# Order of exponentials, penalties and signed scores in the second half's turns of a fused decoder kernel

## What is computed

```python
# top-k self attention, 16 heads of width 8, the 64 best of 128 keys per query
scores = jnp.einsum('bhqd,bhkd->bhqk', q, k) / np.sqrt(D_HEAD)
_, idx = jax.lax.top_k(scores, 64)
logits = jnp.where(knn_mask, scores, -jnp.inf)          # knn_mask set at idx
x = x + out_proj(softmax(logits) @ v)
# channel attention, twice (global, local): q, k, v are scaled and shifted rows
scores = jnp.einsum('bhdn,bhen->bhde', qh, kh) * scale  # 4 heads, 32 x 32 channels
x = x + 2.0 * (att_global + att_local) * wp + bp
# eight experts, all of them on every token
h = jax.nn.silu(x @ wg) * (x @ wu);  acc = acc + h @ wd
```

## Time and profile before

| | us |
|---|---|
| median of three runs | 1395.84 (1394.71 to 1397.26) |
| the profiled execution, its own time | 1398.07 |
| its span in the profile | 1396.3 |
| PE busy | 1046.0 (75%) |
| DVE busy | 961.9 (69%) |
| ACT busy | 679.3 (49%) |
| POOL busy | 474.8 (34%) |

### The profile page before, as it was taken

The page is one execution under the profiler, slowest core; times in us unless marked ns, Lnnn a source line. Parts: engine busy times, 40 slices in busy tenths (PEclk is TensorE's granted clock), DMA queues, the critical chain, the costliest instruction groups (busy, mean ns, idle before and its releaser), DMA issues.

```text
span 1396.3 us, 17900 instructions
## 1 busy us (share of the span) xinstructions
PE 1046.0 (75%) x5079; PEld 690.8 (49%) x5082; DVE 961.9 (69%) x3098; ACT 679.3 (49%) x1774; POOL 474.8 (34%) x461
## 2 busy tenths in 40 slices
PE   5888846655767278877575689778998865888999
PEld 4766713334445145554443344433444444666887
DVE  7555587987577887778878868545668678665332
ACT  4444437433666245665237634265667634633321
POOL 4333347410654144445237500333334403311100
PEclk9999957766878678887577789999998986989999
DMA  4100110000000000000010001011110120222343
GB/s 138 29 23 30 29 32 1 1 0 1 10 22 10 5 18 14 18 9 1 1 54 1 1 22 61 23 46 50 54 46 23 50 76 23 70 90 77 122 147 116
DMA packets 41762, 53.88 MB, mean 39 GB/s; under 512 B 6448, under 2 KB 20672, under 8 KB 41664
## 3 DMA queue, kind: packets, MB, share of 16 engines
q1 hardware_dynamic: 41488, 52.24, 12.0%
q0 software_dynamic: 176, 0.53, 0.1%
HBM read 51.71 MB, written 1.05 MB: 38 GB/s over the span
## 4 chain that ended last, share of the span: by engine, by line
PE 48%; DVE 28%; ACT 9%; issue 7%; POOL 6%; DVEq 1%; DMA 0%; POOLq 0%; SPq 0%; ACTq 0%
PE psum L1739 7%; PE psum L1750 6%; PE psum L1725 6%; PE psum L1816 2%; PE psum L1508 2%; PE psum L1484 2%; PE psum L1603 2%; PE psum L1327 2%; PE psum L1823 2%; PE psum L1466 2%; ACT far L1034 2%; PE psum L1404 2%; PE psum L1557 2%; POOL Wk L711 2%; DVE nmax L2131 1%
## 5 line engine op out<-in xcount | busy, mean ns | idle before, releaser
L2259 DVE TENSOR_TENSOR big<-psum,qe 128x512 f32<-128x512 f32 x106 | 72.9, 688 | 159.8 <-PE psum L1750 76.9
L1187 ACT ACTIVATE qe<-psum 128x512 f32<-128x512 f32 x106 | 62.3, 595 | 127.3 <-PE psum L1739 127.1
L1725 PE MATMUL psum<-big,wexp 128*128 128x256 f32 (+1 forms) x340 | 117.4, 461 | 0.0
L1034 ACT ACTIVATE far<-far,half_far,fmul 128x128 bf16<-128x128 bf16 x256 | 103.0, 488 | 22.9 <-DVE hit L2034 22.9
L2047 DVE MAX8 near<-Wk 128x8 f32<-128x128 f32 x512 | 103.0, 276 | 0.0
L668 POOL TENSOR_SCALAR veps<-mv 128x4 f32<-128x4 f32 x35 | 8.8, 252 | 267.0 <-DVE mv L1953 267.0
L766 POOL TENSOR_TENSOR Wk<-Wk,far 128x1024 f32<-128x1024 f32 x32 | 68.2, 2135 | 70.3 <-ACT far L1034 70.3
L1725 PEld LDWEIGHTS psum<-big,wexp 128*128 128x128 f32 x340 | 70.5, 207 | 31.0 <-issue 22.3
L1750 PE MATMUL psum<-xin,wexp 128*128 128x512 f32 x128 | 70.0, 630 | 13.7 <-DVE far L2259 8.3
L1404 PE MATMUL psum<-ident,Wk 128*128 128x128 f32 x256 | 48.6, 360 | 42.1 <-POOL Wk L711 39.3
L1739 PE MATMUL psum<-xin,wexp 128*128 128x512 f32 x128 | 77.7, 693 | 2.4 <-DVE vaug L2699 1.5
(11 more groups left out here) (359 smaller groups left out, 2867.5 us busy)
## 6 DMA issues: line engine op xcount, KB each, us to landing
wexp<-in_mg SPq DMA_DIRECT2D x48, 256.0 KB, 2.6
wexp<-in_mu SPq DMA_DIRECT2D x48, 256.0 KB, 3.0
wexp<-in_md SPq DMA_DIRECT2D x48, 256.0 KB, 3.1
w<-in_aw SPq DMA_DIRECT2D x8, 256.0 KB, 2.8
w<-in_w2a SPq DMA_DIRECT2D x8, 256.0 KB, 2.6
wqkv<-in_aw SPq DMA_DIRECT2D x8, 192.0 KB, 2.2
ctxt<-in_ctx SPq DMA_DIRECT2D x5, 256.0 KB, 4.2
xin<-in_x SPq DMA_DIRECT2D x4, 256.0 KB, 2.9
```

What stands on the lines that cost most here:

```text
L1034: ins = act.activation(far[t][:, hd, :], far[t][:, hd, :], ACT.Identity, bias=half_far[:, 0:1], scale=fmul[t][:, hd:hd + 1])
L1187: act.activation(sg_of[k >= EARLY][k % 2], bank(5 + k % 2), ACT.Silu).then_inc(silu_done, 1)
L1725: mm = pe.matmul(bank(4)[:, 0:w], wd[l % 2][:, c + j, :], hid_of[k >= EARLY][k % CH][:, j * w:(j + 1) * w], start=first and j == 0, stop=l ...
L2259: dve.tensor_tensor(hid_of[k >= EARLY][k % CH], bank(U_BANK[k]), sg_of[k >= EARLY][k % 2], ALU.mult).then_inc(hu_done, 1)
```

## The change

Five edits, all in turns 7 to 17. (1) `hidden` of the chunk of point 0 moves from point 2 to point 3. (2) On ACT, penalties leave points 0, 1 and 2 (six, six and four heads) and go to points 3 to 6, four heads each, behind `scores_out` of point 5 and ahead of that point's SiLU; the exponentials at points 1 and 2 so come right behind the maxima. (3) On POOL, `less_penalties` moves from points 3 and 4 to points 6 and 8. (4) In the turns with a pair's channel attention and penalties (12 and 14), `signed_scores` moves from point 0 to point 2 and waits for the queries' last step, `c_q`. (5) In the channel attention of the pairs, keys are scaled and shifted at r = -5 and -4, the row of line 823 is added at r = 6 in place of 4; for pairs 2, 3 and 4 the product of queries and keys moves from r = 5 to 4, its maximum and difference from 6 to 5, its exponential from 6 to 4 (point 2, ahead of the SiLU of the chunk of point 0). No arithmetic is changed.

```diff
@@ -157,7 +157,7 @@
 def hidden_point(t):
     if t < START2:
         return t + 1
-    return t if t >= TURNS * PTS else t + 2 if t % PTS < 2 else t + 1
+    return t if t >= TURNS * PTS else t + 3 if t % PTS < 2 else t + 1
 
 
 CHUNK_AT = chunk_points()
@@ -767,14 +767,18 @@
 
             def topk(b, p, half):
                 lo, hi = RANGES[half]
-                if p == 0 and lo <= b < hi:
+
+                pair = next((g for g in range(2, NG) if CH_START[g] == (b - 1) * PTS + 10), None)
+                if p == (0 if pair is None else 2) and lo <= b < hi:
+                    if pair is not None:
+                        pool.wait_ge(c_q, 4 * pair + 4)
                     signed_scores(b)
                 if p == 2 and lo <= b + 2 < hi and b + 2 > lo:
                     spread_keys(b + 2)
                 if p == 3 and lo <= b - 1 < hi:
                     spread_queries(b - 1)
-                if p in (3, 4) and lo <= b < hi:
-                    less_penalties(b, p - 3)
+                if p in (6, 8) and lo <= b < hi:
+                    less_penalties(b, (p - 6) // 2)
                 if p == 10 and lo <= b < hi:
                     maxima_in_parts(b)
 
@@ -804,7 +808,9 @@
 
             def channel(g, r):
                 x, w = x_of[g], GROUPS[g][1]
-                if r == 0:
+
+                key_scaled, key_shifted, based = (0, 2, 4) if g <= 1 else (-5, -4, 6)
+                if r == key_scaled:
                     if g == 0:
                         pool.wait_ge(ew_in, 32)
                     pool.wait_ge(ctxp_in, 16 * (g + 1))
@@ -814,11 +820,11 @@
                         pool.tensor_tensor(chk[k][:, 0:w, :], ctxp_of[g], bc(rowe[:, 4 + 2 * k, :], w), ALU.mult).then_inc(c_k, 1)
                 if r == 1:
                     post_rsqrt(2 * g + 1, w)
-                if r == 2:
+                if r == key_shifted:
                     for k in range(2):
                         pool.wait_ge(c_k, 4 * g + k + 1)
                         pool.tensor_tensor(chk[k][:, 0:w, :], chk[k][:, 0:w, :], bc(rowe[:, 5 + 2 * k, :], w), ALU.add).then_inc(c_k, 1)
-                if r == 4:
+                if r == based:
                     pool.wait_ge(n_h, 2 * g + 1)
                     pool.tensor_tensor(x, x, bc(rowe[:, 9, :], w), ALU.add).then_inc(c_xb, 1)
                 if r == 7:
@@ -1057,10 +1063,10 @@
                     maxima(b - 1)
                 if p in (1, 2) and lo <= b - 2 < hi:
                     exponentials(b - 2, p - 1)
-                if p in (0, 1, 2) and lo <= b < hi:
-                    penalties(b, (range(0, 6), range(6, 12), range(12, H))[p])
                 if p in (5, 7) and lo <= b + 1 < hi:
                     scores_out(b + 1, (p - 5) // 2)
+                if p in (3, 4, 5, 6) and lo <= b < hi:
+                    penalties(b, range(4 * (p - 3), 4 * (p - 2)))
                 if p in (8, 9, 10, 11) and lo <= b + 1 < hi:
                     signs(b + 1, range(4 * (p - 8), 4 * (p - 7)))
 
@@ -1173,7 +1179,7 @@
                         act.wait_ge(base_done, 4 * HALVES)
                     for k in range(2):
                         act.activation(chv_of[g][k], ctxTp[:, 0:w, :], ACT.Identity, bias=cole[:, 2 * k + 1:2 * k + 2], scale=cole[:, 2 * k:2 * k + 1]).then_inc(c_v, 1)
-                if r == 6:
+                if r == (4 if 1 < g < NG - 1 else 6):
                     act.wait_ge(c_sub, g + 1)
                     act.activation(se[:, 0:2 * w, :], se[:, 0:2 * w, :], ACT.Exp, scale=float(P) ** -0.5).then_inc(c_exp, 1)
                 if r == 11:
@@ -1689,7 +1695,7 @@
                     pe.wait_ge(ctxp_in, 16 * (g + 1))
                     pe.wait_ge(n_x, NX_AT["project", g])
                     transposes(bank(X_BANK[g]), ctxp_of[g], ident[:, :], cT_mm, 1, w)
-                if r == 5:
+                if r == (4 if 1 < g < NG - 1 else 5):
                     pe.wait_ge(c_q, 4 * g + 4)
                     pe.wait_ge(c_k, 4 * g + 4)
                     pe.wait_ge(cT_out, g + 1)
@@ -2225,7 +2231,7 @@
                     for k in range(2):
                         dve.wait_ge(c_q, 4 * g + k + 1)
                         dve.tensor_tensor(chq[k][:, 0:w, :], chq[k][:, 0:w, :], row(2 * k + 1), ALU.add).then_inc(c_q, 1)
-                if r == 6:
+                if r == (5 if 1 < g < NG - 1 else 6):
                     dve.wait_ge(c_s_mm, g + 1)
                     dve.tensor_reduce(mx, sc, AX.X, ALU.max).then_inc(c_wgt, 1)
                     dve.wait_ge(c_wgt, 5 * g + 1)
```

## The result

The changed kernel takes 1386.55 us (median of 4 runs, 1383.25 to 1389.93) against 1395.74 for the kernel before: a ratio of 0.9934, 95% interval 0.9915 to 0.9953. It is faster by 9.2 us, where 5.8 were forecast; the time is inside the range. The profiled execution took 1389.93 (span 1388.2), 3.4 above that median. In the changed kernel the lines shown before stand 4 to 6 further down (L1499 is L1505, L1699 is L1705, L1750 is L1756, L2190 is L2196, L2259 is L2265), and L766 stays.

The account below looks back on a forecast made before the run. A plain turn was taken as TensorE's work plus a VectorE and GpSimd tail, other turns adding a middle wait. Terms -1.9 + 4.5 - 0.2 - 3.4 + 1.6 + 2.4 + 4.0 - 1.7 + 0.5 = 5.8 gain: 1390.0 us, range 1377 to 1399.

Parts of the forecast that it names:

- Turn 13 (gain 2.4): Four penalties leave the SiLU's way: TensorE's 1.72 wait shrinks to 0.15, 1.6 slow clock goes; GpSimd meets thresholds for 0.8.
- Turn 14 (gain 4.0): Queries' wait 4.45 and 2.0 slow clock go, less 1.0 new wait, 0.45 late SiLU, 1.0 for half the 2.1 hold.
- Turn 12: Gain 1.6: earlier queries and up-product give 4.1, less 0.45 late SiLU and 2.1 normalization held by GpSimd's second subtraction.
- Turns 10 and 11 (loss 1.7 each): GpSimd's second subtraction meets VectorE's threshold steps: later by 0.4 + 2.0, less 0.69 slack; head wait near 4.7.
- Turn 9 (loss 0.2): An earlier SiLU for point 0 gains 1.4; GpSimd's subtraction meeting VectorE loses 1.6.
- Turn 7 (loss 1.9): Chunk of point 0 multiplied behind the scaling of group 1's queries, so TensorE's next up-product starts 1.9 later.
- Turn 15 (loss 1.7): GpSimd waits for group 4's key load, subtractions and key steps queue behind and hold VectorE's thresholds; marking begins 1.7 later.
- Turn 16 (gain 0.5): No penalties; the channel's exponential ahead of the SiLU costs TensorE a little and frees VectorE of six replacements; gain 0.5.
- The rest (0): Outside turns 7 to 16, nothing gained or lost; what is gained before is kept after turn 17.
- the clock decides: Rival: nine waits each cost one slow chunk of 1.8, so 10 slower, 1406; half of it 1398; chance 0.13.
- It does nothing: Rival: heads set the pace, slack in VectorE's tail eats the middle gains; -2 to +2, 1395; chance 0.16.
- the meeting costs nothing: Rival: VectorE isn't held beside GpSimd's subtraction; gain 19.6, so 1376.2; chance 0.26, wholly or in most turns.

Follow-up runs that it names:

- the subtraction kept apart: Changed kernel, but GpSimd's second subtraction waits until VectorE has marked the dropped keys or written the second normalization; 1376.02 us, 0.9846 of the kernel before.
- the channel's part: Changed kernel with the moves of penalties and subtractions undone, the chunk of point 0 still multiplied at point 3; alone 0.9987 of the kernel before.
- The repair: Changed kernel, but in turn 7 alone the chunk of point 0 is multiplied at point 2 again; 0.9889 of the kernel before.
- both repairs: Changed kernel with turn 7's chunk of point 0 back at point 2 and the second subtraction behind VectorE's tail; 1373.98 us, 0.9841 of the kernel before.
- maxima first: Changed kernel with turn 7's chunk back at point 2, the second subtraction delayed, and VectorE's maxima ahead of the head outputs; 0.9836 of the kernel before.

## Why the prediction was right, and where it was not

**Sign and mechanism** came from the right places: the gain in turn 8 to a tenth, that in turn 13, and the losses from GpSimd's second subtraction meeting VectorE, which the subtraction kept apart shows to be some 10 us. That the sum came so near (8.1 between the spans of the two traces, 9.2 between the medians, for 5.8) is in part luck: the parts miss by up to 3.3 either way, 1.3 of the gain lies ahead of any edit, and the same kernel traced again was 3.5 shorter in S.

**Turn 13 (gain 2.4)** gave 4.0 without the pause. The wait went as forecast (1.72 to 0.18), and the wait for the late hidden chunk at its end grew by the 0.8 forecast (2.92 to 3.76). But busy time fell by 3.3 where I had 1.6: the head of the turn, where I had put nothing, was fast as well, behind waits of 1.02 and 0.40 instead of 2.44 (its first gate-product took 1.08 instead of 2.02).

**Turn 14 (gain 4.0)** is the step that failed most: 0.9 came. The queries' wait went as forecast, 4.45 to 0 with 0.91 of new wait. But for the end I took half of the 2.1; the trace has the whole hold, and the reciprocal root held by the marking too, 3.44 against 0.67, and three slow products of 1.91 after it. The root's part is the near tie in the starts and not the change: in the second trace, with the root free as in the kernel before, the wait was 2.79, and the turn gained 2.8. The meeting's part, 2.1 of wait, is what I had halved. **Turn 12** has the same 2.1: 3.47 against 1.34, the root held in both kernels.

**What the wait of turns 12 and 14 rested on** was misread: I gave it to the signed scores alone. The rows of the kernel before show the two queries' steps held by the subtractions as well; so I priced the signed scores' move at what the subtractions' move brings too (1.16 of the 4.45 is left without the channel's part).

**Turns 10 and 11 (loss 1.7 each)**: 0.8 and 0.3, with a head wait of 3.92 where I had 4.7. The hold was there, but 1.36 instead of 2.0, since the step that I had named, now L2076, began 0.05 ahead of the subtraction, which took 2.35 for its 2.12, and it was L2080 that met it.

**Turn 9 (loss 0.2)** gained 1.3: L2075 was held 1.8 and the head wait rose by 1.2 to 4.19, but TensorE's wait of 0.93 for the first SiLU went, and the clock was 1.00 instead of 0.94, with 21.4 us of busy TensorE instead of 23.0.

**Turn 7 (loss 1.9)** was mis-sized: the wait grew by 2.4 and the turn by 3.0. The repair gave 3.3 there; what of it lasts to the end is open, and beside the subtraction kept apart it was nothing.

**Turn 15 (loss 1.7)**: the mechanism came line by line, with 3.2 of held time. Its cost shows as a new wait of TensorE, 2.58 ahead of L1756 at 1224.01; against it stand 1.5 of the penalties' wait (1.71 to 0.18) and 1.3 of busy time at a clock of 0.95 instead of 0.90, so the turn was 0.3 shorter. **Turn 16 (gain 0.5)** gave 2.5, with a clock of 0.91 against 0.83.

**The rest (0)** lost 3.3 to the clock alone: busy time of the same 560 instructions rose from 108.2 to 111.5. Of the rivals, *the clock decides* was right that slow stretches move about with a change of waits; that each longer wait costs one, as its price had it, the runs don't bear out (turn 10, behind a head wait of 4.19 instead of 2.96, was busy for 31.5 us as before). *It does nothing* fell with the interval, and *the meeting costs nothing* with the subtraction kept apart.

## What to carry to other kernels

List what the other engine does beside every two-tile instruction of VectorE before and after a move: a GpSimd instruction taken off one such place lands beside another, and here a single wait that kept it off all of them was worth 0.6 to 0.9%, about as much as the change. When a wait has several causes, test each part alone, and once more with the other losses taken out: the channel's part seemed to be worth nothing until then. Judge an edit by the stretch from an unedited point to the next, over more than one trace: what it gives in its own turn can be gone two turns later. And look for near ties in the starts of two engines, which can fall either way in the same kernel, before comparing two traces.

## What the runs showed of the hardware

- VectorE and GpSimd hold each other, and whichever is second loses the rest of the first one's instruction: the queries' products, the normalization and even 128x16 steps are held by a 128x1024 subtraction (0.17 becomes 1.53); a 128x2 power is held by a 128x2048 compare (0.71 becomes 2.87), and a subtraction begun beside that compare takes 3.63 instead of 2.12. A reduction (L2078, 0.42) begun inside the subtraction wasn't held. At starts within 0.02 us, the power was held at the end of turn 14 in seven traces of 13 and not in six, and at the end of turn 12 in all.
- The granted clock of identical code with identical waits differs between executions and neighbours: turn 17 to the end takes 114.7, 116.3 or 118.0, in steps of 1.6 to 1.7. A head wait of 2.43 was followed by products at 1.08 (turn 15, both repairs) and one of 1.59 by products at 2.02 (maxima first), so the length of the wait alone doesn't tell the clock behind it.
